# Sums of squares of the queries as one row that a transfer spreads, the last chunk's output products by heads, and the router weights' remainder ahead of GpSimd's

## The chip, the cores and the metric

The program runs on one core of a Trainium2 chip. Its time is the device time in microseconds (us) of one execution; three runs of the kernel before are shown. Less is better. The engines are TensorE (PE; PEld is its weight load), VectorE (DVE), ScalarE (ACT), GpSimd (POOL) and SyncE (SP, which here only issues transfers).

## The reference

Two layers, each cross attention and a feed-forward part, over x of 8 samples, 256 tokens, 512 features. The change lies in the second layer's attention and at the start of its feed-forward part:

```python
q = (hidden_states @ Wq + bq).reshape(b, s, NH, HD).transpose(0, 2, 1, 3)   # NH 16 heads, HD 128
k = (encoder_hidden_states @ Wk + bk) ...                                   # NKV 4 groups
q = _rmsnorm(q, qn_w)          # q * rsqrt(mean(q * q, -1) + 1e-6) * w
scores = jnp.einsum('bhsd,bhed->bhse', q, k) * scale
probs = softmax(scores)
out = jnp.einsum('bhse,bhed->bhsd', probs, v)
return out.transpose(0, 2, 1, 3).reshape(b, s, NH * HD) @ Wo
...
logits = x @ router_w.T        # the feed-forward part: 8 experts, two for each token, and a shared one
```

## The kernel before, in words

The matmuls of this attention work on float32 values that are split in two: a rounded part `hi` (float32r) and the remainder `lo`. A product is three matmuls (`matmul3`, L78 to L80: hi by lo, lo by hi, hi by hi). ScalarE makes each `hi`, VectorE or GpSimd each `lo` by a subtraction.

`ffn0_attention1` holds the first layer's feed-forward part and the second layer's attention. In the attention the 2048 tokens (16 tiles of 128) are taken in 4 chunks of 512, and the 16 heads in 4 groups of 4. The loop runs over u from 0 to 63: the groups outermost, then the chunks, then the 4 heads of the group. A head is one u; four of them make one chunk's turn in one group, after which the output is projected and added to X. There are 16 such turns, called chunks below.

Each engine's instructions stand in an order written out by hand, each behind the semaphores that it waits for. Work is staggered. At step u TensorE does: the transposes of the probabilities of head u (`transposed`, L1750), the sums of squares of head u + 2 (`square_sums`, L1718; ahead of the transposes where u is a multiple of 4), the queries of head u + 3 (`queries`, 12 matmuls of 512 columns), the scores of head u + 2 (12 of 256), the output of head u (`output`, 12 of 256), and at every fourth head the projection (`project`, 48 of 512). The projection writes to the banks that the transposes use (`ptb`), so the transposes of the next head wait until VectorE has added the last tile to X (L1560, semaphore s_added).

The path of the squares: the queries of a head lie in a PSUM bank, features on partitions, tokens in columns. ScalarE squares them (a_sq, L1360) and rounds them (a_q_hi, L1361); VectorE takes the remainder (a_q_lo, L1515). TensorE then takes each 128 columns of a_sq as weights against one column of ones, so that four matmuls (eight instructions, since they are plain float32) give the sums with tokens on partitions. VectorE copies them (a_ssq, L1520), GpSimd raises them to the power -1/2 (a_rq, L1224), and VectorE needs a_rq to scale the scores (L1528). It then takes the maxima (L1535); ScalarE the exponentials (L1367), VectorE divides (L1544), TensorE transposes, ScalarE and VectorE split the result (L1373, L1549), and TensorE multiplies by V. At every eighth head ScalarE rounds new weights (L1333 or L1341, 128x2048), and GpSimd takes their remainder (L1228 or L1234), issues the next load of weights and takes the remainder of the keys (L1241).

`feed_forward1` begins with `norm` of four tiles, then the remainder of the router's weights (L2469), both on VectorE, while GpSimd takes the remainders of the first expert's weights (L2059, L2080).

## Time and profile before

| | us |
|---|---|
| three runs: median (lowest to highest) | 1813.54 (1813.4 to 1814.91) |
| the profiled execution, its own time | 1817.25 |
| its span in the trace | 1815.5 |
| busy in the span: TensorE | 1740.2 (96%) |
| busy: VectorE | 1213.7 (67%) |
| busy: ScalarE | 851.2 (47%) |
| busy: GpSimd | 583.5 (32%) |

The profiled execution is 1.75 above its span and 3.7 above the median of the runs. The attention loop runs from 651 to 1306 in the trace. Busy time counts matmuls as the profile models them, so that matmuls that overlap are counted once; where the next one starts tells how long one holds the engine.

### The profile page before, as it was taken

The numbers are of one execution on the slowest core, as the hardware profiler recorded it, in microseconds if no ns is written. First come the engines' busy times: TensorE is split into PE (matmuls) and PEld (weight loads), VectorE is DVE, ScalarE is ACT, GpSimd is POOL, SyncE is SP. The second block draws the span as 40 slices with busy tenths as digits, with TensorE's granted clock in tenths as the row PEclk, the third lists the DMA queues.
The fourth block names the chain that finished last, engine by engine and source line by source line (L and its number), as shares of the span: only waits on it lengthen the run. The fifth ranks groups of instructions, "written<-read, shape, count | busy, mean of one in ns | idle before, by whom it ended". The sixth has DMA issues, their size and how long they took to land. (4 is left out here: it accounts for less than half of the span.)

```text
span 1815.5 us, 26738 instructions
## 1 busy us (share of the span) xinstructions
PE 1740.2 (96%) x9946; PEld 1443.8 (80%) x9966; DVE 1213.7 (67%) x2313; ACT 851.2 (47%) x1624; POOL 583.5 (32%) x441
## 2 busy tenths in 40 slices
PE   7999998996999989999999999999799999999998
PEld 6998997773444578888888888888667799999876
DVE  5444442895888777767777777777657567676555
ACT  4443432654565564445555555544341256566411
POOL 3111143224686531212132121211110245555342
PEclk9999998998999999999999999999899999999999
DMA  8323211853233761212232221110161488898573
GB/s 313 94 81 105 70 48 33 304 203 99 59 72 91 176 211 59 82 58 82 71 119 73 76 82 59 59 59 1 40 255 49 156 266 273 266 293 258 199 243 110
DMA packets 166346, 238.12 MB, mean 131 GB/s; under 512 B 42054, under 2 KB 103238, under 8 KB 164038
## 3 DMA queue, kind: packets, MB, share of 16 engines
q1 hardware_dynamic: 156620, 203.14, 34.4%
q0 software_dynamic: 9600, 33.30, 5.9%
q8 instruction: 80, 1.31, 0.3%
q14 instruction: 46, 0.38, 0.1%
HBM read 184.24 MB, written 43.78 MB: 126 GB/s over the span
## 5 line engine op out<-in xcount | busy, mean ns | idle before, releaser
L1224 POOL TENSOR_TENSOR a_rq<-a_ssq,a_qhalf 128x4 f32<-128x4 f32 x64 | 65.1, 1017 | 404.7 <-DVE a_ssq L1520 404.7
L1373 ACT ACTIVATE a_pT_hi<-bank 128x512 fp32r<-128x512 f32 x128 | 69.5, 599 | 186.1 <-PE bank L1750 185.9
L78 PE MATMUL bank<-a_xT_hi,a_wq_lo 128*128 128x512 f32 (+1 forms) x384 | 143.9, 375 | 1.4 <-DVE a_xT_lo L503 1.4
L1367 ACT ACTIVATE a_scores<-a_scores,a_nmax 128x256 f32<-128x256 f32 x256 | 127.2, 503 | 27.4 <-DVE a_nmax L1535 27.3
L80 PE MATMUL bank<-a_xT_hi,a_wq_hi 128*128 128x512 f32 (+1 forms) x384 | 138.3, 360 | 0.0
L79 PE MATMUL bank<-a_xT_lo,a_wq_hi 128*128 128x512 f32 (+1 forms) x384 | 138.1, 360 | 0.0
L78 PE MATMUL bank<-a_wo_hi,a_oT_lo 128*128 128x512 f32 x320 | 126.8, 396 | 2.9 <-DVE a_oT_lo L552 1.3
L2059 POOL TENSOR_TENSOR e_wg_lo<-raw_g,e_wg_hi 128x1408 fp32r<-128x1408 f32 x26 | 91.2, 3508 | 112.9 <-ACT e_wg_hi L2126 112.9
L1528 DVE SCALAR_TENSOR_TENSOR a_scores<-bank,a_rq,a_mask 128x256 f32<-128x256 f32 x256 | 106.1, 477 | 28.7 <-PE bank L80 20.4
L79 PE MATMUL bank<-a_wo_lo,a_oT_hi 128*128 128x512 f32 x320 | 124.9, 390 | 0.0
L80 PE MATMUL bank<-a_wo_hi,a_oT_hi 128*128 128x512 f32 x320 | 124.9, 390 | 0.0
L78 PE MATMUL bank<-a_pT_hi,a_V_lo 128*128 128x256 f32 x384 | 111.1, 289 | 8.1 <-DVE a_pT_lo L1549 6.3
L1260 POOL TENSOR_TENSOR f_h<-f_vv,f_gs 128x512 f32<-128x512 f32 x64 | 93.3, 1461 | 62.5 <-DVE f_vv L1465 61.8
L1560 DVE TENSOR_TENSOR X<-X,bank 128x512 f32<-128x512 f32 x64 | 43.8, 687 | 101.4 <-PE bank L80 101.4
L79 PE MATMUL bank<-a_pT_lo,a_V_hi 128*128 128x256 f32 x384 | 110.2, 287 | 0.0
L80 PE MATMUL bank<-a_pT_hi,a_V_hi 128*128 128x256 f32 x384 | 110.1, 287 | 0.0
L1549 DVE TENSOR_TENSOR a_pT_lo<-bank,a_pT_hi 128x512 fp32r<-128x512 f32 x128 | 82.1, 682 | 18.0 <-ACT a_pT_hi L1373 17.9
L1544 DVE TENSOR_SCALAR a_scores<-a_scores,a_rden 128x256 f32<-128x256 f32 x256 | 85.9, 399 | 2.3
L78 PEld LDWEIGHTS bank<-a_pT_hi,a_V_lo 128*128 128x128 f32 x384 | 75.1, 196 | 10.0 <-DVE a_oT_lo L1554 6.9
L80 PEld LDWEIGHTS bank<-a_xT_hi,a_wq_hi 128*128 128x128 f32 x384 | 73.7, 192 | 11.1
L78 PEld LDWEIGHTS bank<-a_xT_hi,a_wq_lo 128*128 128x128 f32 x384 | 74.1, 193 | 10.3 <-DVE a_xT_lo L503 1.8
L1535 DVE TENSOR_REDUCE a_nmax<-a_scores 128x2 f32<-128x512 f32 x128 | 81.2, 675 | 0.0
(416 smaller groups left out, 5326.2 us busy)
## 6 DMA issues: line engine op xcount, KB each, us to landing
raw_g<-in_egw SPq DMA_DIRECT2D x26, 704.0 KB, 4.7
raw_u<-in_euw SPq DMA_DIRECT2D x26, 704.0 KB, 6.2
a_xT_hi<-x1T_hi SPq DMA_DIRECT2D x16, 1024.0 KB, 6.1
a_xT_lo<-x1T_lo SPq DMA_DIRECT2D x16, 1024.0 KB, 8.5
raw_d<-in_edw SPq DMA_DIRECT2D x26, 512.0 KB, 5.9
y_routed<-m_y SPq DMA_DIRECT2D x39, 256.0 KB, 6.3
raw_d<-in_edw SPq DMA_DIRECT2D x26, 192.0 KB, 6.8
a_cTraw<-in_ctxT SPq DMA_DIRECT2D x8, 512.0 KB, 6.0
```

Source lines behind the costliest of these rows:

```text
L78: pe.matmul(out, w[1], x[0], start=first, stop=False)
L79: pe.matmul(out, w[0], x[1], start=False, stop=False)
L80: return pe.matmul(out, w[0], x[0], start=False, stop=last)
L1224: pool.tensor_tensor(rq[:, h % HG, :], ssq[:, h % HG, :], qhalf[:], ALU.pow).then_inc(s_rq, 1)
L1260: pool.tensor_tensor(h[n % 2][:, j * 512:(j + 1) * 512], vv[u % 2][:], gs[u % 2][:], ALU.mult).then_inc(s_h, 1)
L1367: act.activation(row, row, ACT.Exp, bias=nmax[:, i % 2, t:t + 1], accum_out=den[:, i % 2, t:t + 1]).then_inc(s_exp, 1)
L1373: act.activation(pT[b].hi[:], ptb[b][:].rearrange("p (k s) -> p k s", k=QT), ACT.Copy).then_inc(ft.hi, 1)
L1528: dve.scalar_tensor_tensor(sc[i % 2][:, r, :], scb[b][:, t * S:(t + 1) * S], rq[:, i % HG, r:r + 1], mask[:, t, :], ALU.mult, ALU.add).the ...
L1535: dve.tensor_reduce(nmax[:, i % 2, b * QT:(b + 1) * QT], sc[i % 2][:, b * QT:(b + 1) * QT, :], AX.X, ALU.max, negate=True).then_inc(s_nmax, 1)
L1544: dve.tensor_scalar(row, row, rden[:, i % 2, t:t + 1], None, ALU.mult).then_inc(s_p, 1)
L1549: dve.tensor_tensor(pT[b].lo[:], ptb[b][:].rearrange("p (k s) -> p k s", k=QT), f32(pT[b].hi[:]), ALU.subtract).then_inc(ft.lo, 1)
L2059: pool.tensor_tensor(pairs[w % 2].g.lo[:], raws[raw_of(w)].g[:], f32(pairs[w % 2].g.hi[:]), ALU.subtract).then_inc(s_glo, 1)
```

## The change

1. The sums of squares. The squares are themselves split: ScalarE rounds them (a_sq_hi), VectorE takes the remainder (a_sq_lo), and TensorE multiplies a single column of ones as weights by both, two matmuls of 512 columns that leave the sums as one row on one partition. ScalarE adds the epsilon and writes the row to SBUF (a_sum_row), with its columns laid so that four tokens of a partition stand together; then it issues a transfer that spreads the row over 128 partitions (a_ssq). GpSimd waits for that transfer. The sums of head u + 3 are taken at step u, between the two halves of the output of head u, and VectorE takes queries' and squares' remainders ahead of the scores.
2. The last chunk. Its projection (`project_last`) writes to banks of its own and is cut by heads: the first two heads' products ahead of the output of head 62, the third's on both sides of the output of head 63, the fourth's at the end.
3. The last layer. VectorE takes the remainder of the router's weights after one `norm` instead of four; GpSimd takes each of its first two remainders in four pieces.

```diff
         V = [first.V, over.pair("a1_V", [P, CT, HD])]
         over = Region(nc, keep.slab)
         q = [over.pair(f"a1_q{j}", [P, C]) for j in range(2)]
+        sq_lo = Region(nc, over.offset)
+        sq_lo = [sq_lo.take(f"a1_sq_lo{j}", [P, C], F32R) for j in range(2)]
         sq = [over.take(f"a1_sq{j}", [P, C]) for j in range(2)]
         K = [first.K, over.pair("a1_K", [P, C])]
...
 
         sb = lambda name, shape, dt=F32: mem.take("a1_" + name, shape, dt)
         bqg = [first.bqg, sb("bqg", [P, HG])]
-        ssq = sb("ssq", [P, HG, CT])
+        ones_r, sum_eps = sb("ones_r", [P, 1], F32R), sb("sum_eps", [P, 1])
+        ssq = [sb(f"ssq{j}", [P, CT]) for j in range(2)]
         qhalf = sb("qhalf", [P, CT])
...
 
             def rstd(u, h):
 
-                pool.wait_ge(s_ssqc, u + 1)
-                pool.tensor_tensor(rq[:, h % HG, :], ssq[:, h % HG, :], qhalf[:], ALU.pow).then_inc(s_rq, 1)
+                pool.wait_ge(s_col[u % 2], u // 2 * 16 + 16)
+                pool.tensor_tensor(rq[:, h % HG, :], ssq[u % 2][:], qhalf[:], ALU.pow).then_inc(s_rq, 1)
 
             def wq_lo(g):
...
 
             def queries(u, g, i, begin=False):
                 act.wait_ge(fq.mm, u + 1)
-                if not begin:
-                    act.wait_ge(s_ssq, u - 1)
                 if g:
                     act.wait_ge(s_bqg, g)
                 b = bqg[g % 2][:, i % HG:i % HG + 1]
+                after(act, s_ssq, u - 1)
                 act.activation(sq[i % 2][:], qb[i % 2][:], ACT.Square, bias=b).then_inc(s_sq, 1)
                 act.activation(q[i % 2].hi[:], qb[i % 2][:], ACT.Identity, bias=b).then_inc(fq.hi, 1)
+                after(act, s_ssq, u)
+                act.wait_ge(s_sq, u + 1)
+                act.activation(sq_hi[:], sq[i % 2][:], ACT.Copy).then_inc(s_sqhi, 1)
+
+            def square_sums(u):
+                act.wait_ge(s_ssq, u + 1)
+                if u:
+                    act.wait_ge(s_col[(u - 1) % 2], (u - 1) // 2 * 16 + 16)
+                act.activation(sum_row[0:1, :].rearrange("a (p t) -> a t p", t=CT),
+                               ssb[0:1, :].rearrange("a (t p) -> a t p", t=CT), ACT.Identity,
+                               bias=sum_eps[0:1, :]).then_inc(s_row, 1)
+                act.wait_ge(s_row, u + 1)
+                after(act, s_rq, u - 1)
+                act.dma_start(ssq[u % 2][:], sum_row[0:1, :].rearrange("a (p t) -> a p t", t=CT)).then_inc(s_col[u % 2], 16)
 
             def exp(u, i):
...
                         keys_hi(n + 1)
                     if i % HG == 1:
                         values_hi(n + 1)
+                if u + 3 < G * U:
+                    square_sums(u + 3)
                 output(u, n, i)
 
...
                 dve.scalar_tensor_tensor(q[i % 2].lo[:], qb[i % 2][:], bqg[u // U % 2][:, i % HG:i % HG + 1],
                                          f32(q[i % 2].hi[:]), ALU.add, ALU.subtract).then_inc(fq.lo, 1)
 
-            def square_sums(u, i):
-                dve.wait_ge(s_ssq, u + 1)
-                dve.tensor_scalar(ssq[:, i % HG, :], ssb[:, 0:CT], HD * RMS_EPS, None, ALU.add).then_inc(s_ssqc, 1)
+            def squares(u, i):
+                dve.wait_ge(s_sqhi, u + 1)
+                dve.tensor_tensor(sq_lo[i % 2][:], sq[i % 2][:], f32(sq_hi[:]), ALU.subtract).then_inc(s_sqlo, 1)
 
...
                 for t in range(CT):
                     dve.wait_ge(s_out, n * CT + t + 1)
                     row = X[:, c * CT + t, :]
-                    dve.tensor_tensor(row, row, ptb[t % 2][:], ALU.add).then_inc(s_added, 1)
+                    of = banks[t] if n == G * NC - 1 else ptb[t % 2]
+                    dve.tensor_tensor(row, row, of[:], ALU.add).then_inc(s_added, 1)
 
             def statistics(n, t):
...
             normalise(0, 0)
             for u in range(G * U):
                 i, n = u % U, u // HG
-                if u + 2 < G * U:
-                    square_sums(u + 2, i + 2)
                 transposed(u)
                 if u + 1 < G * U:
                     normalise(u + 1, i + 1)
+                if u + 3 < G * U:
+                    queries(u + 3, i + 3)
+                    squares(u + 3, i + 3)
                 if u + 2 < G * U:
                     scores(u + 2, i + 2)
-                if u + 3 < G * U:
-                    queries(u + 3, i + 3)
-                if u + 2 < G * U:
                     maxima(u + 2, i + 2)
                 if n > (G - 1) * NC:
...
                 last.then_inc(fq.mm, 1)
 
             def square_sums(u, i):
-                pe.wait_ge(s_sq, u + 1)
+                pe.wait_ge(s_sqlo, u + 1)
                 if u == 0:
                     pe.wait_ge(s_xTc, T)
-                after(pe, s_ssqc, u)
-                for t in range(CT):
-                    last = pe.matmul(ssb[:, t:t + 1], sq[i % 2][:, t * P:(t + 1) * P], ones[:, 0:1], start=True,
-                                     stop=True)
-                last.then_inc(s_ssq, 1)
+                    pe.wait_ge(s_const, 3)
+                after(pe, s_row, u)
+                pe.matmul(ssb[0:1, :], ones_r[:], sq_hi[:], start=True, stop=False)
+                pe.matmul(ssb[0:1, :], ones_r[:], sq_lo[i % 2][:], start=False, stop=True).then_inc(s_ssq, 1)
 
             def scores(u):
...
                 if u == 0:
                     pe.wait_ge(s_fadded, T)
                 after(pe, fo.lo, u)
-                for b in range(NB):
+                for b in halves:
                     pe.wait_ge(ft.lo, u * NB + b + 1)
                     for k in range(QT):
                         last = matmul3(pe, ob[:, b * S:(b + 1) * S], part(v, slice(None), b * QT + k),
                                        part(pT[b], slice(None), k), k == 0, k == QT - 1)
-                last.then_inc(fo.mm, 1)
+                if NB - 1 in halves:
+                    last.then_inc(fo.mm, 1)
 
             def project(u, n):
...
                                 last.then_inc(s_out, 1)
+
+            def project_last(heads, tiles):
+
+                pe.wait_ge(fo.lo, G * U - HG + heads[-1] + 1)
+                for t in tiles:
+                    for k in heads:
+                        last = matmul3(pe, banks[t][:], part(oT, slice(None), k, slice(t * P, (t + 1) * P)),
+                                       part(wo, slice(None), k), k == 0, k == HG - 1)
+                    if HG - 1 in heads:
+                        last.then_inc(s_out, 1)
 
             x_transposed(0)
...
             next_xT(T - 1)
             for u in range(G * U):
                 g, i, n = u // U, u % U, u // HG
-                if i % HG == 0 and u + 2 < G * U:
-                    square_sums(u + 2, i + 2)
                 transposed(u, n, i)
-                if i % HG and u + 2 < G * U:
-                    square_sums(u + 2, i + 2)
                 if u + 3 < G * U:
                     queries(u + 3)
                 if u + 2 < G * U:
                     scores(u + 2)
-                output(u)
-                if i % HG == HG - 1:
+                if u == G * U - 2:
+                    pe.wait_ge(s_masked, G * U * CT)
+                    project_last(range(HG - 2), range(CT))
+                if u == G * U - 1:
+                    project_last(range(HG - 2, HG - 1), range(CT // 2))
+                output(u, range(1))
+                if u + 3 < G * U:
+                    square_sums(u + 3, i + 3)
+                output(u, range(1, NB))
+                if u == G * U - 1:
+                    project_last(range(HG - 2, HG - 1), range(CT // 2, CT))
+                    project_last(range(HG - 1, HG), range(CT))
+                elif i % HG == HG - 1:
                     if i == HG - 1:
                         pe.wait_ge(s_wolo, g + 1)
...
             pool.affine_select(out=before[:], in_=ones[:], compare_op=ALU.is_gt, fill=0.0, base=0,
                                pattern=[[1, P]], channel_multiplier=-1).then_inc(s_const, 1)
             pool.tensor_tensor(fold[:], ident[0:2 * E, 0:E], ident[0:2 * E, E:2 * E], ALU.add).then_inc(s_fold, 1)
-            gate_lo(0)
+            pool.wait_ge(s_ghi, 1)
+            for k in range(KD):
+                ins = pool.tensor_tensor(pair0.g.lo[:, k, :], raw0.g[:, k, :], f32(pair0.g.hi[:, k, :]), ALU.subtract)
+            ins.then_inc(s_glo, 1)
             pool.wait_ge(s_uhi, 1)
-            pool.tensor_tensor(pair0.u.lo[:], raw0.u[:], f32(pair0.u.hi[:]), ALU.subtract).then_inc(s_ulo, 1)
+            for k in range(KD):
+                ins = pool.tensor_tensor(pair0.u.lo[:, k, :], raw0.u[:, k, :], f32(pair0.u.hi[:, k, :]), ALU.subtract)
+            ins.then_inc(s_ulo, 1)
             pool.wait_ge(s_ve, 1)
             pool.tensor_tensor(rstd[:, T - CT:T], last.ve[:, T - CT:T], last.mhalf[:, T - CT:T], ALU.pow).then_inc(s_rstd, 1)
...
                 step(dve.tensor_tensor(tokf[:], tokf[:], tb[0][:, NT:2 * NT], ALU.add))
                 dve.tensor_copy(token[:], tokf[:]).then_inc(s_tok, 1)
 
-            for t in chunk(0):
-                norm(t)
+            norm(0)
             dve.wait_ge(s_rw, 1)
             dve.tensor_tensor(rw2[:, :, E:2 * E], rw[:], f32(rw2[:, :, 0:E]), ALU.subtract).then_inc(s_rw, 1)
+            for t in range(1, CT):
+                norm(t)
             transposed(0)
             transposed(1)
```

The order of the instructions on three engines, read from the two programs; L numbers of the changed kernel are its own.

VectorE, inside the attention loop (`ffn0_attention1`), the steps of one head of the kernel before, from the scores of one head to the output of the previous:

```order
L1528 SCALAR_TENSOR_TENSOR a_scores_4403<-bank,a_rq,a_mask 128x256 x4
L1515 SCALAR_TENSOR_TENSOR a_q_lo<-bank,a_bqg,a_q_hi 128x512
L1535 TENSOR_REDUCE a_nmax<-a_scores_4403 128x2 x2
L1554 TENSOR_TENSOR a_oT_lo<-bank,a_oT_hi 128x512
L1520 TENSOR_SCALAR a_ssq<-bank 128x4
L1549 TENSOR_TENSOR a_pT_lo<-bank,a_pT_hi 128x512 x2
L1540 RECIPROCAL a_rden<-a_den 128x4
L1544 TENSOR_SCALAR a_scores_4403<-a_scores_4403,a_rden 128x256 x4
```

And in the changed kernel, the same stretch of VectorE:

```order
L1544 SCALAR_TENSOR_TENSOR a_q_lo<-bank,a_bqg,a_q_hi 128x512
L1549 TENSOR_TENSOR a_sq_lo_4410<-a_sq_4412,a_sq_hi 128x512
L1557 SCALAR_TENSOR_TENSOR a_scores_4403<-bank,a_rq,a_mask 128x256 x4
L1564 TENSOR_REDUCE a_nmax<-a_scores_4403 128x2 x2
L1583 TENSOR_TENSOR a_oT_lo<-bank,a_oT_hi 128x512
L1578 TENSOR_TENSOR a_pT_lo<-bank,a_pT_hi 128x512 x2
L1569 RECIPROCAL a_rden<-a_den 128x4
L1573 TENSOR_SCALAR a_scores_4403<-a_scores_4403,a_rden 128x256 x4
```

The copy of the sums (a_ssq) is gone, the remainder of the next queries (a_q_lo) has moved ahead of the scores, and the remainder of their squares (a_sq_lo) stands behind it.

TensorE, the steps of one head in the kernel before (rows of the middle of each run of products left out; a_scores are transposed first, then come the sums, the queries, the scores, the output):

```order
L1750 MATMUL bank<-ident,a_scores_4403 128x128 x8
L1718 MATMUL bank<-ones,a_sq_4411 128x1 x4
L78 MATMUL bank<-a_xT_hi,a_wq_lo 128x512
...
L78 MATMUL bank<-a_K_hi,a_q_lo 128x256
...
L78 MATMUL bank<-a_pT_hi,a_V_lo 128x256
```

And in the changed kernel, from the scores to the next head's transposes:

```order
L78 MATMUL bank<-a_K_hi,a_q_lo 128x256
...
L78 MATMUL bank<-a_pT_hi,a_V_lo 128x256
...
L1747 MATMUL bank<-a_sq_hi,a_ones_r 1x512
L1748 MATMUL bank<-a_sq_lo_4410,a_ones_r 1x512
L78 MATMUL bank<-a_pT_hi,a_V_lo 128x256
...
L1778 MATMUL bank<-ident,a_scores_4402 128x128 x8
```

The sums of squares of head u + 3 now stand between the two halves of the output of head u, eighteen matmuls behind the queries that they are summed from; before, those of head u + 2 stood right behind the transposes, a whole head after their queries.

ScalarE, the steps of one head in the kernel before:

```order
L1379 ACTIVATE a_oT_hi<-bank 128x512
L1373 ACTIVATE a_pT_hi<-bank 128x512 x2
L1367 ACTIVATE a_scores_4402,a_den<-a_scores_4402,a_nmax 128x256 x4
L1360 ACTIVATE a_sq_4410<-bank,a_bqg 128x512
L1361 ACTIVATE a_q_hi<-bank,a_bqg 128x512
```

And in the changed kernel:

```order
L1401 ACTIVATE a_oT_hi<-bank 128x512
L1395 ACTIVATE a_pT_hi<-bank 128x512 x2
L1389 ACTIVATE a_scores_4403,a_den<-a_scores_4403,a_nmax 128x256 x4
L1368 ACTIVATE a_sq_4413<-bank,a_bqg 128x512
L1369 ACTIVATE a_q_hi<-bank,a_bqg 128x512
L1372 ACTIVATE a_sq_hi<-a_sq_4413 128x512
L1378 ACTIVATE a_sum_row<-bank,a_sum_eps 1x4x128
L1383 DMA a_ssq_4428<-a_sum_row 128x1x4
```

Three steps are new: the rounded squares (a_sq_hi), the row of sums out of its bank (a_sum_row), and the issue of the transfer that spreads the row over the partitions.

## Rows read from the trace of the kernel before

**Rows 1.** Windows: stretch and length, busy time of each engine, TensorE clock, DMA.
```profile
655.00:1272.00 617.00, 615.10 (x3842) 548.27 (x3841) 458.62 (x1036) 319.37 (x818) 136.37 (x103) 1.00 0.22 74
```

**Rows 2.** Timeline of TensorE (start, us, engine, line): one head, projection, next head.
```profile
1003.97 1.04 PE L1750 MATMUL bank<-ident,a_scores 128*128 128x128 f32 x8
1004.84 0.95 PE L1718 MATMUL bank<-ones,a_sq 128*128 128x1 f32 x8
1005.65 0.48 PE L78 MATMUL bank<-a_xT_hi,a_wq_lo 128*128 128x512 f32 x1
...
1008.24 0.39 PE L80 MATMUL bank<-a_xT_hi,a_wq_hi 128*128 128x512 f32 x1
1008.47 0.28 PE L78 MATMUL bank<-a_K_hi,a_q_lo 128*128 128x256 f32 x1
...
1011.32 0.40 PE L78 MATMUL bank<-a_wo_hi,a_oT_lo 128*128 128x512 f32 x1
...
1022.63 0.95 PE L1718 MATMUL bank<-ones,a_sq 128*128 128x1 f32 x8
1023.58 1.09 PE L1750 MATMUL bank<-ident,a_scores 128*128 128x128 f32 x8
```

**Rows 3.** Timeline of ScalarE in the head that starts at 1023.58.
```profile
1024.27 1.09 ACT L1373 ACTIVATE a_pT_hi<-bank 128x512 fp32r<-128x512 f32 x2 [12.15 <-PE bank L1750]
...
1027.47 0.69 ACT L1360 ACTIVATE a_sq<-bank,a_bqg 128x512 f32<-128x512 f32 x1 [0.15 <-PE bank L80]
1028.05 0.68 ACT L1361 ACTIVATE a_q_hi<-bank,a_bqg 128x512 fp32r<-128x512 f32 x1
1028.62 0.63 ACT L1346 ACTIVATE a_K_hi<-ahead_ctx 128x512 fp32r<-128x512 f32 x1
```

**Rows 4.** Timeline of VectorE around the same head.
```profile
1022.15 1.38 DVE L1560 TENSOR_TENSOR X<-X,bank 128x512 f32<-128x512 f32 x2 [4.48 <-PE bank L80]
...
1027.56 1.14 DVE L1544 TENSOR_SCALAR a_scores<-a_scores,a_rden 128x256 f32<-128x256 f32 x4
...
1030.54 0.74 DVE L1515 SCALAR_TENSOR_TENSOR a_q_lo<-bank,a_bqg,a_q_hi 128x512 fp32r<-128x512 f32 x1
1031.20 1.27 DVE L1535 TENSOR_REDUCE a_nmax<-a_scores 128x2 f32<-128x512 f32 x2
```

**Rows 5.** Groups of instructions: count, then busy time and mean ns of one.
```profile
L2285 DVE TENSOR_TENSOR e_wd_lo<-raw_d,e_wd_hi 96x512 fp32r<-96x512 f32 x25 | 16.9, 678 | 0.0
```

**Rows 6.** Timeline of SyncE: start and length of one DMA issue.
```profile
1030.65 0.34 SPq L1144 DMA_DIRECT2D ahead_ctx<-K  x1
```

**Rows 7.** DMA issues: count, KB each, median us to landing.
```profile
r_rw<-in_rwT SPq DMA_DIRECT2D x1, 16.0 KB, 1.8
ahead_ctx<-K SPq DMA_DIRECT2D x16, 256.0 KB, 5.6
```

**Rows 8.** Timeline of GpSimd at two starts of eight heads.
```profile
660.37 4.61 POOL L1234 TENSOR_TENSOR a_wo_lo<-ahead_raw,a_wo_hi 128x2048 fp32r<-128x2048 f32 x1 [7.52 <-ACT a_wo_hi L1341]
...
666.12 1.30 POOL L1241 TENSOR_TENSOR a_K_lo<-ahead_ctx,a_K_hi 128x512 fp32r<-128x512 f32 x1
...
1159.88 1.05 POOL L1224 TENSOR_TENSOR a_rq<-a_ssq,a_qhalf 128x4 f32<-128x4 f32 x1
```

**Rows 9.** Timeline of VectorE at the same two places.
```profile
664.46 3.11 DVE L1544 TENSOR_SCALAR a_scores<-a_scores,a_rden 128x256 f32<-128x256 f32 x4
...
1158.10 2.49 DVE L1544 TENSOR_SCALAR a_scores<-a_scores,a_rden 128x256 f32<-128x256 f32 x4
```

**Rows 10.** One line of ScalarE: duration ns min/median/max, first and last start.
```profile
L1333 ACT ACTIVATE a_wq_hi<-ahead_raw x3: 1917/1917/1920, 740.6 to 1069.7; 128x2048 fp32r<-128x2048 f32 x3
```

**Rows 11.** Timeline of TensorE in the last three heads: its waits.
```profile
1287.48 0.55 PE L78 MATMUL bank<-a_pT_hi,a_V_lo 128*128 128x256 f32 x1 [4.06 <-DVE a_pT_lo L1549]
```

**Rows 12.** Timelines of VectorE and GpSimd at the start of the last layer.
```profile
1309.63 3.17 DVE L2469 TENSOR_TENSOR r_rw<-r_rw,r_rw 128x32 fp32r<-128x32 f32 x1
...
1309.36 3.40 POOL L2059 TENSOR_TENSOR e_wg_lo<-raw_g,e_wg_hi 128x1408 fp32r<-128x1408 f32 x1 [0.50 <-ACT e_wg_hi L2126]
```

34 lines of the change are left out of this document (24 added, 10 removed).

## The prediction

> **What bounds the kernel now.** I read the page first, then the stretch of the attention loop, then one head on each engine. TensorE is busy in 615.1 of the 617 us of the loop and its clock stands at 1.00, that is 2.4 GHz [rows 1], so there the time is what TensorE issues, and any wait that it gets is added in full. The timeline shows one head: transposes at 1003.97, sums of squares at 1004.84, queries at 1005.65, scores at 1008.47, output behind them, projection at 1011.32 [rows 2]. A head is 1011.32 - 1003.97 = 7.35, of it the sums 0.81, the twelve matmuls of the queries 2.82 (0.235 each), scores and output 2.85 together; both are twelve matmuls of 256 columns, so 1.43 each. The projection is 1022.63 - 1011.32 = 11.31. A chunk is 4 x 7.35 + 11.31 + 0.14 (the sums take 0.95 where they come first) = 40.85. In the last three heads there are true waits, 4.06 the longest [rows 11].
>
> **The sums themselves.** Removed: 0.81 a head (0.95 in a chunk's first). Added: two matmuls of 512 columns. With one column as weights they are not in the trace; I take the 0.235 of a 512-column matmul with 128, so 0.47. Bounds: 0.2 if half went by, 0.81 if plain float32 were the nearer row. TensorE's own work falls by 0.34 a head, 22 over 64 heads.
>
> **The wait that comes with them.** Now the sums of head u + 3 stand eighteen matmuls behind its queries, and they need the remainder of the squares. I count from E, the end of the last matmul of the queries, 1008.24 + 0.39 = 1008.63 [rows 2]. The scores start at 1008.47 and take 1.43, half an output 0.71: TensorE reaches the sums at 1010.61, E + 1.98. The chain beside it: ScalarE starts the squares about 0.05 after a matmul ends (the hand-over in the other direction is as short: the last addition ends at 1022.15 + 1.38 = 1023.53, the transposes start at 1023.58 [rows 2, 4]); a_q_hi starts 0.58 behind the squares and takes 0.68 [rows 3], so it ends at E + 1.31. VectorE's a_q_lo starts at E + 1.36, the next instruction follows 0.66 later [rows 4], and a_sq_lo, a subtraction in SBUF, takes 0.68 [rows 5]: E + 2.70. With 0.1 for the weight load ahead of the matmul, E + 2.80. The rounding of the squares on ScalarE (0.63, as a_K_hi from SBUF, behind 0.57 of a_q_hi [rows 3]) ends at E + 1.8 and decides nothing. So TensorE waits 2.80 - 1.98 = 0.82 in each head, with every engine free in time. Behind it on TensorE stand the second half of the output and the next transposes, and ScalarE and VectorE wait for those, so nothing catches it up. Bounds 0.6 to 1.0, from hand-overs of 0 to 0.1. A head becomes 7.35 - 0.81 + 0.47 + 0.82 = 7.83.
>
> **The chunk's first head.** Its transposes wait for the last addition, which ends at 1023.53 [rows 4]; today the sums (1022.63 to 1023.58 [rows 2]) fill just that time. With the sums gone from there the wait is bare: 0.95, no gain. A chunk is 0.95 + 4 x 7.83 + 11.31 = 43.58, that is 2.73 more.
>
> **The issue on ScalarE.** ScalarE must wait for its own row (0.68, as the other steps with a bias [rows 3]), then issue the transfer. No row has an issue on ScalarE; SyncE's shortest near here is 0.34 [rows 6], GpSimd's issues cost more, and the lower bound is nothing. I take 0.34. From the start S of the sums: they end at S + 0.63, the row ends at S + 1.36, the issue at S + 1.75, a_oT_hi holds ScalarE 0.5 more, so a_pT_hi starts at S + 2.25. It could have started 0.69 (1024.27 - 1023.58) behind the transposes [rows 2, 3], which start at S + 0.47 + 0.71, so at S + 1.87: 0.38 late. From a_pT_hi to the end of the division takes 1027.56 + 1.14 - 1024.27 = 4.43 [rows 3, 4], and a_q_lo stands behind it; this way it starts about 0.25 later than by the queries. That adds 0.25 to three heads of a chunk, 0.75. A chunk is then 44.3, 3.5 more; over fifteen chunks +52. Nothing for the issue gives +41; an issue of 0.8 gives +21 more.
>
> **Every eighth head.** GpSimd's subtraction of new weights, the load and the keys hold it from 660.37 to 667.42, 7.05 in all [rows 8], and VectorE's division there takes 3.11 instead of 1.14, ending 0.15 behind GpSimd [rows 9]. Today this costs TensorE some tenths, since the probabilities are needed a head later. Afterwards the squares stand behind that division. Counted from the transposes: the rounding of the weights (1.92 [rows 10]) starts at 5.7, GpSimd goes from 7.6 to 14.7, the next head's division is due at 7.83 + 3.98 = 11.8 [rows 2, 4] and is held to 14.7; 0.8 for its rest, 0.66, 0.68 and 0.1 bring the squares to 16.9, where TensorE wants them at 7.83 + 6.65 = 14.5. That is 2.4; less about 0.3 that I grant for today's cost it is 2.1, seven times: +15. Bounds 0 to 4 each.
>
> The Trainium skill, SBUF - State Buffer, "Who interferes with whom", says that a VectorE instruction with two SBUF inputs contends with a GpSimd instruction that reads SBUF, and that the later one is blocked until the other ends. The trace agrees: 3.17 us for 32 columns beside GpSimd's 3.40 [rows 12]. By that rule a_sq_lo could also be held by a_rq, once a head.
>
> **The transfer.** Its 2 KB have no like here. The column's transfer starts at S + 1.75; VectorE wants a_rq behind a_sq_lo, about 6.7 behind the next transposes, S + 7.9. Less 1.05 of a_rq [rows 8], 5.1 is left for landing. Rows bound it by 1.8 (16 KB) and 5.6 (256 KB) [rows 7]; it is nearer in size to the first. Cost nothing; past 5.1 it is charged.
>
> **The ends.** In the last chunk 24 matmuls (5.6) of the projection go where the 4.06 wait is, less 1.6 that they overshoot and 1.4 (a_oT_hi and its remainder ahead of the last head's products), with a lesser wait filled: about -2 (0 to -5). The router's remainder leaves the shadow of GpSimd's 3.40 and drops from 3.17 to 0.2, part of it on the path: -2.5 (0 to -4). The loop's start I leave at 0, between -3 and +3.
>
> **Sum.** 52 + 15 - 2 - 2.5 = +62.5. The profiled execution took 1817.25, which gives 1879.8; it stands 3.7 above the median, so 1876.
>
> **Rivals.**
> *Cheap edges*: the issue costs ScalarE nothing and the eighth heads half: +62.5 - 11 - 7.5, about 1857. For it: most issues have no engine waiting; against it: ScalarE here has a wait on itself ahead. It shares the forecast's mechanism.
> *A late column or a blocked remainder*: a landing of 8 us in the one head of a chunk beside the 2 MB loads puts VectorE 2.9 late, of which some 0.9 is slack: 2 x 15 = +30, 1906. If a_rq held a_sq_lo or the division for its full 1.0 in each head, 61 more, 1937. Against the last: at a later start the divisions ended at 1160.59 while a_rq ran from 1159.88 to 1160.93 [rows 8, 9], so it did not hold them.
> *Faster, the remainder is hidden*: if a_sq_lo were ready by E + 1.98, the chain being 0.82 shorter than its rows, a head is 7.01 and a chunk 0.95 + 28.0 + 11.31 = 40.3, 0.55 less than now: -8, and -4.5 at the ends, 1801. It needs hand-overs and durations below every row; the sign turns where the wait is under about 0.2 and issue and eighth heads cost nothing.
> *The change does nothing measurable*: 1813, only by chance between these.
>
> **How the numbers follow.** Forecast 0.68, cheap edges 0.15, late or blocked 0.12, faster 0.03, no change 0.02. The time is the forecast's, 1876. The range: below, cheap edges with waits of 0.66 instead of 0.82 (-10), 1847; above, an issue of 0.8, 1897, widened to 1900. So slower 0.95, within 0.2% 0.02, faster 0.03; 0.2% (3.6 us) is about what a measurement can tell here.
>
> **What would show it.** TensorE's wait ahead of the first sums matmul, put down to a_sq_lo, near 0.8 in chunk-first heads and near 1.1 in the others, 50 to 70 us in all; the sums 0.23 apart; a chunk of about 44.3, every second 2.5 longer; transposes of each chunk's first head waiting 1.0 for X. Wrong, if those waits are missing, if a_ssq lands past 5 us, or if TensorE's clock falls from 1.00 at waits this short.

## The result, and the profile after

| | runs | median, us (lowest to highest) |
|---|---|---|
| before | 4 | 1814.22 (1813.4 to 1815.51) |
| after | 4 | 1913.1 (1911.03 to 1917.66) |

The ratio is 1.0547, with a 95% interval of 1.0533 to 1.0561: 99 us more, where the prediction had 62.5 more and a range that ended at 1900. The span of the profiled execution is 1912.6.

The stretch of the attention loop, in the view that [rows 1] show for before (length, then busy time of PE, PEld, DVE, ACT and POOL, the clock, DMA), from the changed kernel:

```profile
660.00:1365.00 705.00, 607.05 (x3437) 512.25 (x3437) 488.04 (x1027) 410.86 (x927) 139.72 (x103) 0.97 0.20 63
```

TensorE now has 98 us without work in this stretch, and its clock is no longer at 1.00 throughout. The chain of waits in the loop says for what (engine and line that waited, releaser, us in total, times, longest):

```profile
POOL a_rq L1232 <- DMA a_ssq<-a_sum_row: 365.0, 56, 19.8
...
ACT a_sum_row L1378 <- PE bank L1748: 89.7, 54, 3.5
PE bank L1747 <- DVE a_sq_lo L1549: 89.6, 62, 4.0
DVE a_rden L1569 <- ACT a_scores L1389: 64.7, 62, 1.3
...
ACT a_oT_hi L1401 <- ACT a_sum_row L1378: 30.8, 54, 0.6
...
PE bank L1778 <- DVE X L1590: 11.7, 15, 0.8
...
DVE a_scores L1557 <- POOL a_rq L1232: 3.0, 3, 1.9
```

The second to fourth lines are three engines waiting for one another in turn: TensorE for the remainder of the squares, ScalarE for TensorE's sums, VectorE for ScalarE's exponentials. GpSimd's 365 us for the column are idle time of an engine that nobody waits for: VectorE waited for a_rq only 3.0 us in all. TensorE's timeline, the sums in a chunk's first and second head and in its fourth (start, us, engine, line; the wait is in brackets):

```profile
1043.94 0.39 PE L1747 MATMUL bank<-a_sq_hi,a_ones_r 128*1 128x512 f32 x1 [0.61 <-DVE a_sq_lo L1549]
...
1054.81 0.59 PE L1747 MATMUL bank<-a_sq_hi,a_ones_r 128*1 128x512 f32 x1 [3.74 <-DVE a_sq_lo L1549]
...
1073.45 0.39 PE L1747 MATMUL bank<-a_sq_hi,a_ones_r 128*1 128x512 f32 x1 [1.52 <-DVE a_sq_lo L1549]
1073.68 0.40 PE L1748 MATMUL bank<-a_sq_lo,a_ones_r 128*1 128x512 f32 x1
```

The last pair, 1.52, is what the second to fourth heads of an ordinary chunk show. The line ahead of it, 3.74, stands in the second head of a chunk in which GpSimd takes the remainder of new weights; the matmul behind it takes 0.59 instead of 0.39. ScalarE in the same fourth head:

```profile
1070.65 0.68 ACT L1368 ACTIVATE a_sq<-bank,a_bqg 128x512 f32<-128x512 f32 x1
1071.22 0.69 ACT L1369 ACTIVATE a_q_hi<-bank,a_bqg 128x512 fp32r<-128x512 f32 x1
1071.79 0.64 ACT L1372 ACTIVATE a_sq_hi<-a_sq 128x512 fp32r<-128x512 f32 x1
1074.12 1.18 ACT L1378 ACTIVATE a_sum_row<-bank,a_sum_eps 1x512 f32<-1x512 f32 x1 [1.69 <-PE bank L1748]
1075.32 0.48 ACTq L1383 DMA_DIRECT2D a_ssq<-a_sum_row  x1
1075.84 0.60 ACT L1401 ACTIVATE a_oT_hi<-bank 128x512 fp32r<-128x512 f32 x1 [0.55 <-ACT a_sum_row L1378]
```

The row, 512 numbers on one partition, takes 1.18, not the 0.68 of the other steps with a bias [rows 3], and its issue 0.48. From the starts of TensorE's transposes (L1778; before L1750) come the lengths of heads and chunks, worked out by subtraction for this kernel and for those of the experiments. The prediction's "every eighth head" is the third column: every second chunk, in whose first head ScalarE rounds 128x2048 new weights and GpSimd takes their remainder. Its range covers five such chunks; the first and the thirteenth (47.2 in the changed kernel, 40.9 before) are apart:

```
                     heads of an ordinary chunk   chunk   a chunk with GpSimd's   first
                     (fourth: with projection)            large remainders        chunk
before               6.57  7.41  7.41  19.67      41.07   41.2                    43.5
after                7.76  8.70  8.65  20.90      46.0    49.6                    52.5
row written plainly  7.76  8.17  8.12  20.37      44.4    48.8 to 50.0            47.8
issue by SyncE       7.76  7.93  7.92  20.15      43.75   49.0 to 50.5            52.8
sums later           7.06  8.68  8.63  20.86      45.2    47.5 to 48.3            51.2
no remainder         6.78  6.74  6.75  18.99      39.3 *  42.0                    42.2
pieces               7.78  8.71  8.64  20.88      46.0    49.9 to 51.3            51.4
four moves           7.06  7.10  7.07  19.32      40.5    45.9 to 47.9            49.6
  and spread         7.07  7.08  7.07  19.30      40.5    41.6 to 42.6            44.0
  no rem. and spread 6.79  6.78  6.75  19.03      39.35   39.3 to 40.2            42.0
  the same, earlier  6.79  6.78  6.75  19.03      39.35   39.3                    41.4
* 39.3 to 40.2
```

The fifteen chunks up to head 60 are together 97.1 longer than before, and so are the spans (1912.6 - 1815.5): the loss lies in the loop. Eight ordinary chunks are 4.9 to 5.1 longer, five with large remainders 8.4 to 8.5, the first 9.1, the thirteenth 6.3.

### The profile page after: what moved, and what is told of

Read it like the earlier page. It is cut to its first block and busy times, and to the rows that moved or that the text cites. A ratio compares the mean times of both kernels' runs of the same rounds, so it can differ in the third digit from the quotient of the medians.

```text
span 1912.6 us, 26422 instructions
## 1 busy us (share of the span) xinstructions
PE 1739.3 (91%) x9562; PEld 1410.8 (74%) x9582; DVE 1245.4 (65%) x2313; ACT 953.2 (50%) x1753; POOL 588.3 (31%) x448
## 3 DMA queue, kind: packets, MB, share of 16 engines
q8 instruction: 78, 1.28, 0.3%
## 5 line engine op out<-in xcount | busy, mean ns | idle before, releaser
L1378 ACT ACTIVATE a_sum_row<-bank,a_sum_eps 1x512 f32<-1x512 f32 x64 | 76.2, 1190 | 89.7 <-PE bank L1748 89.7
L1747 PE MATMUL bank<-a_sq_hi,a_ones_r 128*1 128x512 f32 x64 | 26.6, 415 | 90.7 <-DVE a_sq_lo L1549 90.7
L1778 PE MATMUL bank<-ident,a_scores 128*128 128x128 f32 x512 | 74.1, 292 | 14.3 <-DVE X L1590 11.7
```

What stands on the lines that cost most here:

```text
L1378: act.activation(sum_row[0:1, :].rearrange("a (p t) -> a t p", t=CT), ssb[0:1, :].rearrange("a (t p) -> a t p", t=CT), ACT.Identity, bias= ...
L1778: last = pe.transpose(ptb[b][:, k * S + t * P:k * S + (t + 1) * P], sc[i % 2][:, r, k * P:(k + 1) * P], ident[:])
```

## The experiments

Theory A is the prediction's: TensorE waits for a_sq_lo, and what ScalarE does for the row stands ahead of a_oT_hi and a_pT_hi, so that an edge there comes round to the next head's squares. Theory B is that the transfer of the column, or GpSimd's power of -1/2 behind it (a_rq), is late. Theory C is that GpSimd's hold on VectorE and the slower clock make most of the loss. All runs are given beside runs of the kernel before on the same chip (1814.5, 1817.5, 1815.2 and 1815.4 us in the four groups).

**The other two parts alone** (the kernel before with `project_last`, the router's order and GpSimd's pieces).

> The kernel before with the change's other two parts alone: the last chunk's output products split by heads, and the router's remainder ahead of GpSimd's pieces; the sums of squares stay as they were. Both theories on the loss lay it on the sums, so both expect this kernel slightly under the kernel before: the forecast's terms were -2 (0 to -5) for the tail and -2.5 (0 to -4) for the router, so 1810 us against 1814, ratio 0.9975. If the two parts cost something that the loop hid, it would be at or over 1814.

Measured: 1810.71 us, ratio 0.9986 (0.9975 to 0.9996), so these parts gain 0.7 to 4.5 us (0.0004 to 0.0025 of 1814). The loss is the sums' alone. The router's remainder, which took 3.17 beside GpSimd [rows 12], takes 0.28 now; the line is the changed kernel's:

```profile
L2520 DVE TENSOR_TENSOR r_rw<-r_rw,r_rw 128x32 fp32r<-128x32 f32 x1 | 0.3, 278 | 0.0
```

**The row written plainly.**

```diff
-act.activation(sum_row[0:1, :].rearrange("a (p t) -> a t p", t=CT),
-               ssb[0:1, :].rearrange("a (t p) -> a t p", t=CT), ACT.Identity,
+act.activation(sum_row[0:1, :].rearrange("a (p t) -> a p t", t=CT),
+               ssb[0:1, :].rearrange("a (t p) -> a p t", t=CT), ACT.Identity,
```

> The changed kernel with the row written as it comes and the bank read in steps of four elements' order instead (the same row lands in the same place in the buffer; only which side of ScalarE's instruction has the stride is changed). Theory A (what ScalarE does for the row stands ahead of a_oT_hi, and each part of it is paid in three heads of four): if the strided write made the row 1.19 us instead of 0.68, the row falls by 0.51 and 47 heads by as much: 1913 - 24 = 1889 us. If the row stays at 1.19, the stride of the write is not the cause, and the time stays at 1913. Theory B (the column's landing or the power behind it is late): the row ends 0.5 us earlier and nothing else changes, so the time stays at 1913 whatever the row takes. Theory C (GpSimd's hold and the clock): 1913 too.

Measured: 1898.88 us, ratio 1.0468 (1.0451 to 1.0486). The group of the row, of this kernel and then of the changed one (count, busy time, mean ns of one, idle time ahead):

```profile
L1378 ACT ACTIVATE a_sum_row<-bank,a_sum_eps 1x512 f32<-1x512 f32 x62 | 42.0, 678 | 96.0 <-PE bank L1748 96.0
```

```profile
L1378 ACT ACTIVATE a_sum_row<-bank,a_sum_eps 1x512 f32<-1x512 f32 x62 | 73.9, 1191 | 89.7 <-PE bank L1748 89.7
```

678 ns against 1191: the write in steps of 16 bytes costs 0.51 us; a read of PSUM in steps of 512 bytes costs nothing. Second, third and fourth heads are 0.53 shorter each, first heads not at all, as theory A says; for theory B nothing should have moved. A chunk is 44.4, and the forecast with 0.68 for the row was 44.3. Of the 24 us expected 14 came (22 in the profiled execution, the shortest of the four): in the chunks with large remainders the gain was lost again, since the first of VectorE's four division steps was held until GpSimd's a_K_lo ended and the fourth until its a_V_lo ended:

```profile
1035.88 4.07 DVE L1573 TENSOR_SCALAR a_scores<-a_scores,a_rden 128x256 f32<-128x256 f32 x4
```

The Trainium skill, SBUF — State Buffer, "Door 1: The DMA port swizzle", states that SBUF has lines of 16 bytes and that each access that crosses to a new line pays a penalty. The trace agrees: the strided write, four float32 apart, takes 1.76 times the plain one (1191 / 678).

**The transfer issued by SyncE.**

```diff
 # ScalarE, square_sums(u): heads 0 to 2 keep their issue there
-act.wait_ge(s_row, u + 1)
-after(act, s_rq, u - 1)
-act.dma_start(ssq[u % 2][:], ...)
 # SyncE
+for u in range(G * U - 3):
+    sp.wait_ge(s_row, u + 4)
+    sp.wait_ge(s_rq, u + 2)
+    sp.dma_start(ssq[(u + 3) % 2][:], ...)
+    ...   # x behind the first head's, K behind the second's, V behind the third's
```

> The changed kernel with the transfers of heads 3 and on issued from SyncE's queue; the loads of keys, values and x that SyncE issues are put between them. Theory A: ScalarE goes from the row straight to a_oT_hi, which stands 0.55 to 0.6 us behind it now; 47 heads are shorter by 0.55 to 0.6: 1913 - 27 = 1886 us. The row itself stays at 1.19. Theory B (the landing is what is late): the column lands at best at the same time, more likely 0.1 to 0.3 us later for the step to another engine, so 1913 to 1925. Theory C: 1913.

Measured: 1891.95 us, ratio 1.0426 (1.0408 to 1.0445). ScalarE now goes on at once:

```profile
1054.44 1.20 ACT L1391 ACTIVATE a_sum_row<-bank,a_sum_eps 1x512 f32<-1x512 f32 x1 [1.58 <-PE bank L1761]
1055.43 0.63 ACT L1414 ACTIVATE a_oT_hi<-bank 128x512 fp32r<-128x512 f32 x1
```

a_oT_hi starts 0.99 behind the row's start, where it stood 1.72 behind it (1075.84 - 1074.12). So waiting for its own row and issuing cost ScalarE 0.73, and the second to fourth heads are shorter by 0.72 to 0.77, the first heads by nothing. That is more than the 0.55 to 0.6 expected: a_oT_hi, which waits for nothing here, starts 0.21 before the row ends (1055.43 against 1055.64). The chunks with large remainders gave some of it back, so that 21 us came instead of 27.

**The sums later on TensorE.**

```diff
-output(u, range(1))
+output(u, range(NB))
 if u + 3 < G * U:
     square_sums(u + 3, i + 3)
-output(u, range(1, NB))
```

> The changed kernel with TensorE's sums behind all six of a head's remaining output products (0.72 us later in its order) instead of ahead of them; ScalarE's order is as it was. If TensorE's wait for a_sq_lo is itself the cost, the products cover it: 0.6 of 15 first heads and 0.72 of 47 others are gained, 1913 - 9 - 34 = 1870 us. Theory A in its full form says that the other heads run in a loop through ScalarE (a_sq_lo, sums, row, issue, a_oT_hi, a_pT_hi, exponentials, squares, a_sq_lo) in which the products have no part: only the first heads of chunks gain 0.6, 1913 - 9 = 1904 us, and TensorE's wait for a_sq_lo shrinks while one of the same size shows elsewhere. Theory B: 1913 or more.

Measured: 1895.46 us, ratio 1.0445 (1.0427 to 1.0463). This run tells the two forms of theory A apart. First heads gain 0.70; the three others gain nothing (8.68, 8.63, 20.86), although six more products now stand ahead of the sums. TensorE's timeline in a fourth head:

```profile
1061.77 0.40 PE L1747 MATMUL bank<-a_sq_hi,a_ones_r 128*1 128x512 f32 x1 [1.50 <-DVE a_sq_lo L1549]
```

The wait is 1.50 as before, just one place later. In these heads the products are not what sets the time. The loop is: a_sq_lo, the sums, the row and its issue, a_oT_hi, a_pT_hi, the exponentials, and from there VectorE's division and a_q_lo to the next a_sq_lo. It closes through VectorE: in the changed kernel's fourth head above, a_sq_hi ends at 1072.43, and a_sq_lo starts behind a_q_lo at 1072.72. The 9 us beyond the 1904 expected lie in the chunks with large remainders, 47.5 to 48.3 instead of 49.6.

**Without the squares' remainder.**

```diff
-act.activation(sq_hi[:], sq[i % 2][:], ACT.Copy)       # ScalarE; a_sq is written rounded now
-dve.tensor_tensor(sq_lo[i % 2][:], sq[i % 2][:], f32(sq_hi[:]), ALU.subtract)
-pe.matmul(ssb[0:1, :], ones_r[:], sq_hi[:], start=True, stop=False)
-pe.matmul(ssb[0:1, :], ones_r[:], sq_lo[i % 2][:], start=False, stop=True)
+pe.matmul(ssb[0:1, :], ones_r[:], sq[i % 2][:], start=True, stop=True)
```

> The changed kernel without the squares' remainder: ScalarE writes the square rounded at once, a_sq_hi and a_sq_lo are gone, and one matmul sums. What it leaves out: the part of each square below TensorE's rounding. The row, its strided write (1.19 us) and its issue stay on ScalarE. Theory A: the sums no longer wait (the square ends before the fourth product), so 1.52 us goes in each of 47 heads, 0.6 in 15 first heads and about 3 in 7 eighth heads: 1913 - 70 - 9 - 20 = 1814 us, about the kernel before, though row and issue still cost what they cost. Theory B (landing and power late): the row is only earlier, and VectorE's scores are not waiting for it now, so 1913. Theory C (GpSimd's hold and the clock): a_sq_lo is one of the instructions that are held, so the eighth heads alone gain: 1913 - 10 to 20.

Measured: 1810.4 us, ratio 0.997 (0.9951 to 0.9988). The row still takes 1186 ns and is still issued by ScalarE, and neither costs anything in ordinary heads now: once a_sq_lo is gone the loop no longer closes and TensorE is the bound. The run takes out more than the loop's edge: one matmul a head (0.23, some 15 us in all), and a step each of ScalarE and VectorE. TensorE's timeline has the sums without a wait and heads of 6.74:

```profile
1031.90 1.04 PE L1773 MATMUL bank<-ident,a_scores 128*128 128x128 f32 x8
1037.69 0.39 PE L1743 MATMUL bank<-a_sq,a_ones_r 128*1 128x512 f32 x1
1038.64 1.04 PE L1773 MATMUL bank<-ident,a_scores 128*128 128x128 f32 x8
```

Theory B is refuted here and theory C as the main cause: this kernel sends the same transfers and has GpSimd's same work.

**GpSimd's large remainders in pieces** (each 128x2048 subtraction of `wq_lo` and `wo_lo` as four of 128x512 behind one another).

> The changed kernel with GpSimd's remainders of 128x2048 (4.6 us each) in four pieces of 128x512 behind one another. The term under test is that of the eighth heads (chunks of 49.6 us beside 46.0, seven of them: 25 us, and the first chunk of 52.5). If VectorE gets in between two pieces, its division and a_sq_lo lose about 1.2 us at most instead of up to 4, the 3.7 us waits fall to 2 and the clock stays up: chunks of 46.5 to 47.5, 1913 - 18 = 1895 us. If pieces behind one another hold VectorE as one instruction does: 1913, and chunks stay at 49.6.

Measured: 1916.81 us, ratio 1.055 (1.0532 to 1.0568). Nothing is gained. VectorE beside the four pieces, then GpSimd:

```profile
1047.46 1.27 DVE L1568 TENSOR_REDUCE a_nmax<-a_scores 128x2 f32<-128x512 f32 x2
1050.35 1.28 DVE L1582 TENSOR_TENSOR a_pT_lo<-bank,a_pT_hi 128x512 fp32r<-128x512 f32 x2
```

```profile
1046.99 5.04 POOL L1245 TENSOR_TENSOR a_wo_lo<-ahead_raw,a_wo_hi 128x512 fp32r<-128x512 f32 x4 [16.10 <-ACT a_wo_hi L1354]
1052.33 0.80 POOL L1249 DMA_DIRECT2D ahead_raw<-in_Wq  x1 [0.30 <-POOL a_wo_lo L1245]
1053.15 1.28 POOL L1253 TENSOR_TENSOR a_K_lo<-ahead_ctx,a_K_hi 128x512 fp32r<-128x512 f32 x1
1054.38 1.10 POOL L1232 TENSOR_TENSOR a_rq<-a_ssq,a_qhalf 128x4 f32<-128x4 f32 x1
1055.46 1.25 POOL L1257 TENSOR_TENSOR a_V_lo<-ahead_ctx,a_V_hi 128x512 fp32r<-128x512 f32 x1
```

The pieces hold nothing: the maxima and a_pT_lo take beside them what they take elsewhere, and the changed kernel's one subtraction of 4.62 us stood beside the same steps. The division comes behind it, and meets the remainders of K and V. Its first step, its first three and all four, from the same timeline with narrower windows:

```profile
1052.89 1.71 DVE L1577 TENSOR_SCALAR a_scores<-a_scores,a_rden 128x256 f32<-128x256 f32 x1
1052.89 2.23 DVE L1577 TENSOR_SCALAR a_scores<-a_scores,a_rden 128x256 f32<-128x256 f32 x3
1052.89 3.98 DVE L1577 TENSOR_SCALAR a_scores<-a_scores,a_rden 128x256 f32<-128x256 f32 x4
```

The first step ends at 1054.60, 0.17 behind a_K_lo; the second and third pass beside a_rq in 0.34 each; the fourth ends at 1056.87, 0.16 behind a_V_lo. By the Trainium skill, SBUF — State Buffer, "Who interferes with whom", the one that is issued second is blocked for the other's whole instruction. The trace agrees: each hold ends with the one instruction of GpSimd that it met, and a_rq holds nothing. So cutting the large subtraction could not help here. What it does is push a_K_lo and a_V_lo back to where VectorE divides and takes a_sq_lo, and four pieces behind one another push them as far (5.04 us against 4.62). Whether pieces hold VectorE less where they do meet it, this run does not show.

**Four moves together**: the three above and the row behind a_oT_hi on ScalarE.

```diff
+output(u, n, i)
 if u + 3 < G * U:
     square_sums(u + 3)
-output(u, n, i)
```

> The changed kernel with the three edits tried singly (the row written plainly, the transfer issued by SyncE, the sums behind the head's last product) and a fourth: the row stands behind a_oT_hi on ScalarE instead of ahead of it. Theory A: with the row out of the loop, TensorE waits only for a_sq_lo, 0.1 us; VectorE's own work of some 7.2 us a head is then the longest; heads of 7.1, 7.3, 7.3 and about 19.6, chunks of 41.3, the eighth ones 3 more: 1814 + 15 x 0.2 + 7 x 3 + 5 = 1843 us. If each saving went with its own singly measured share (-19, -22 and -18), it would be 1913 - 59 = 1854. Theory B: the column lands some 1.2 us later in the head than before this edit, so scores wait for a_rq and the time is over 1880.

Measured: 1853.15 us, ratio 1.0197 (1.018 to 1.0214). Ordinary chunks are 40.5, less than the 41.07 of before: the row is out of the loop, and the heads of 7.1 are now about as long as VectorE's own work, which runs through the second and third without a gap. What is left lies in the chunks with large remainders, 46 to 48, more than expected (1843 us was), and in the fourteenth and fifteenth, 43.6 each, where VectorE also takes the last layer's statistics.

**The four moves without the remainder.**

> The kernel with all four moves, without the squares' remainder as well (left out: the part of each square below TensorE's rounding). Theory A: nothing of the sums stands in TensorE's way; a head has 0.57 us less of products and ScalarE and VectorE have 0.5 and 0.6 less each; TensorE is the bound again, only the wait for X's addition (0.8 to 0.95 in a chunk's first head) is no longer filled by 0.81 us of sums: chunks of 39.4 to 39.9 beside 41.07, some 20 us under the kernel before, about 1790. Theory B: over 1814, since the landing would be late here at the latest.

Measured: 1804.12 us, ratio 0.9925 (0.9905 to 0.9944). Ordinary chunks are 39.35, just under the 39.4 to 39.9 expected; those with large remainders are 40.2 to 42.0, which the expectation of 1790 had left out. Beside the run without the remainder alone, the four moves gain 6 us more.

**GpSimd's remainders spread**: pieces over three heads, each behind that head's a_sq_lo (or a_q_lo).

```diff
+if u + 3 < G * U:
+    pool.wait_ge(s_sqlo, u + 4)
 ...                                   # K's and V's remainders stay here
+pieces = (range(0), range(1), range(1, 3), range(3, 4))[i % HG]
+if i < HG and len(pieces):
+    wo_lo(g, pieces)
+if U // 2 <= i < U // 2 + HG and g + 1 < G and len(pieces):
+    wq_lo(g + 1, pieces)
```

> The kernel with all four moves, and GpSimd's remainders spread: each 128x2048 one in pieces of 128x512 over three heads (one, two, one), and every piece, K's and V's too, behind that head's a_sq_lo, so that it runs beside VectorE's scores and maxima, which read PSUM or were not held in the traces so far. Its chunks without GpSimd's large work are 40.5 us (before: 41.06), the seven with it 46 to 48, the first 49.6. Theory A with GpSimd's hold as the cause of the eighth heads' term: those fall to 40.5 to 42: 1853 - 7 x 5.5 - 5 = 1810 us, under the kernel before by 4. If the term is another one (ScalarE's a_wo_hi of 1.9 us ahead of a_oT_hi, or the slow clock by itself), chunks stay at 44 or over and the time at 1840 or more. Theory B (the landing): 1853, nothing changes for it.

Measured: 1820.49 us, ratio 1.003 (1.002 to 1.0041). The chunks with large remainders fall from 46 to 48 to 41.6 to 42.6: the spread takes away most of their excess over 40.5. Two things went together in it. In the kernel with the four moves VectorE's division and a_sq_lo are held for 22 us in all beside a_K_lo and a_V_lo, here for nothing; and the clock no longer falls. The run does not tell them apart. Two pieces beside VectorE's scores and maxima, of GpSimd and then of VectorE:

```profile
1002.74 2.54 POOL L1260 TENSOR_TENSOR a_wo_lo<-ahead_raw,a_wo_hi 128x512 fp32r<-128x512 f32 x2 [1.56 <-DVE a_sq_lo L1573]
```

```profile
1001.98 0.68 DVE L1573 TENSOR_TENSOR a_sq_lo<-a_sq,a_sq_hi 128x512 fp32r<-128x512 f32 x1
1002.57 1.66 DVE L1581 SCALAR_TENSOR_TENSOR a_scores<-bank,a_rq,a_mask 128x256 f32<-128x256 f32 x4
1004.14 1.27 DVE L1588 TENSOR_REDUCE a_nmax<-a_scores 128x2 f32<-128x512 f32 x2
```

VectorE's durations are those of a head without GpSimd. A stretch of 600 us of this kernel's loop has the clock at 1.00:

```profile
660.00:1260.00 600.00, 574.12 (x3364) 484.45 (x3363) 458.48 (x1005) 374.38 (x921) 137.85 (x123) 1.00 0.23 74
```

It misses the 1810 expected. What it loses against before lies in its fourteenth and fifteenth chunks of 42.9, where VectorE also has the last layer's statistics, and in those with pieces, 0.4 to 1.7 longer than before's; in four of these TensorE waits for the last piece of a_wo_lo (2.9 us in all) and the fourth head takes 20.3 instead of 19.3. That the statistics are the cause was not tried.

**The same spread without the remainder of the squares.**

> The same spread in the kernel with all four moves and without the squares' remainder (left out: the part of each square below TensorE's rounding); the pieces stand behind a_q_lo, there being no a_sq_lo. Its seven chunks of 40.2 to 42.0 should fall to 39.4 to 39.8 as their neighbours: 1804 - 7 x 2.2 - 3 = 1786 us. If GpSimd's hold is not what makes them long: 1804.

Measured: 1794.29 us, ratio 0.9887 (0.9871 to 0.9903), 10 us gained by the spread where 18 were expected. Three of the chunks with pieces are 39.3, three 40.2 to 40.3; in these and in the first the projection waits for the last piece of a_wo_lo (a fourth head of 19.9 to 20.0 instead of 19.0).

**The spread in the kernel as changed, and nothing else.**

> The changed kernel with nothing but that spread of GpSimd's remainders. If GpSimd's hold on VectorE is the term of the eighth heads, their chunks fall from 49.6 to 46.0 to 46.8 and the first from 52.5 to 49: 1913 - 7 x 3.2 - 3 = 1888 us; what is left to 1814 is then theory A's alone, some 4.9 us in each chunk. Theory C (GpSimd's hold and the clock make most of the loss): the time falls by over 50, to 1860 or less.

Measured: 1899.48 us, ratio 1.0457 (1.044 to 1.0474). It gains 14, not 25 and not over 50: theory C is worth this much of the 99. Chunks with large remainders are 46.7 to 47.6, not 49.6.

What made them 49.6 can be read from the changed kernel's trace, here in the second head of one. The rounding of the weights and a_oT_hi on ScalarE, with a_oT_hi of an ordinary chunk's second head:

```profile
1042.91 1.91 ACT L1350 ACTIVATE a_wo_hi<-ahead_raw 128x2048 fp32r<-128x2048 f32 x1
1047.03 0.60 ACT L1401 ACTIVATE a_oT_hi<-bank 128x512 fp32r<-128x512 f32 x1 [0.61 <-ACT a_sum_row L1378]
1095.94 0.60 ACT L1401 ACTIVATE a_oT_hi<-bank 128x512 fp32r<-128x512 f32 x1 [0.61 <-ACT a_sum_row L1378]
```

GpSimd, and VectorE beside it:

```profile
1044.90 4.62 POOL L1242 TENSOR_TENSOR a_wo_lo<-ahead_raw,a_wo_hi 128x2048 fp32r<-128x2048 f32 x1 [16.08 <-ACT a_wo_hi L1350]
1050.64 1.28 POOL L1249 TENSOR_TENSOR a_K_lo<-ahead_ctx,a_K_hi 128x512 fp32r<-128x512 f32 x1
1052.95 1.25 POOL L1253 TENSOR_TENSOR a_V_lo<-ahead_ctx,a_V_hi 128x512 fp32r<-128x512 f32 x1
1050.80 2.07 DVE L1573 TENSOR_SCALAR a_scores<-a_scores,a_rden 128x256 f32<-128x256 f32 x4
1053.45 1.30 DVE L1549 TENSOR_TENSOR a_sq_lo<-a_sq,a_sq_hi 128x512 fp32r<-128x512 f32 x1
```

The window behind the wait of 3.74, in which TensorE's clock is 0.50, that is 1.2 GHz:

```profile
1054.80:1059.80 5.00, 4.99 (x19) 4.39 (x20) 4.27 (x9) 3.23 (x6) 0.72 (x1) 0.50 0.31 96
```

Counted from the head's transposes (1045.12; 1094.65 in the ordinary chunk), a_oT_hi starts at 1.91 instead of 1.29: 0.62 late. The division takes 0.93 longer, held by a_K_lo; a_sq_lo takes 0.62 longer, held by a_V_lo; and at the lower clock TensorE needs 2.09 instead of 1.18 from the sums to the next transposes (1056.90 - 1054.81). Together 3.1, the head's 11.8 against 8.7. The third head is 0.5 longer, its first products still at the lower clock.

**Pieces a head earlier.** `(range(1), range(1, 2), range(2, 4), range(0))`.

> The kernel with all four moves, the spread and no remainder of the squares (left out as before: the part of each square below TensorE's rounding), with one change more: GpSimd's pieces of the large remainders stand in the chunk's first three heads (one, one, two) instead of the second to fourth, so that the products of the output weights no longer wait for the last piece. In the trace of the kernel with pieces in the second to fourth heads that wait is 4.6 us in four places, and four of its fourth heads take 20.0 instead of 19.0. Expected: those four fall by 0.9 to 1.0, 1794 - 4 = 1790 us; if the earlier pieces hold VectorE in a first head instead, where ScalarE already rounds weights for 1.9 us, it stays at 1794.

Measured: 1789.2 us, ratio 0.9853 (0.9837 to 0.987), as expected and the fastest here. The second to thirteenth chunks are 39.3, the fourteenth and fifteenth 40.2. It leaves out the squares' remainder; of the kernels that keep it, only the one with the two other parts alone is under the kernel before.

## Why the prediction was right in kind and short in size

- **The sums themselves**: right. L1747 and L1748 start 0.23 apart, 0.46 a head for the two.
- **The wait for a_sq_lo**: 0.82 forecast for every head with the engines free in time; 0.61 where that holds, in first heads (a head of 7.76 to 7.82 against the forecast's 7.83).
- **The chunk's first head**: its transposes wait for X bare, as forecast (0.78 on TensorE in 15 chunks, with the weight load ahead of it).
- **The issue on ScalarE: this is the step that failed, in its size.** It took "0.68, as the other steps with a bias" for the row and 0.34 for the issue, and made 0.25 in three heads of it. The row took 1.19 and the issue 0.48 on ScalarE; the second and third heads are 0.85 to 0.94 longer than the first, where 0.25 + 0.51 + 0.14 makes 0.90. The wait for a_sq_lo in these heads was 1.5, not the 1.1 that the prediction named. The mechanism stood: with the row at 0.68 a chunk was 44.4 (forecast 44.3), with it at 1.19 it is 46.0. Over fifteen chunks an ordinary chunk's excess is 15 x 4.93 = 74 where 52 was forecast: 22 of the 34.6 us missed. The bound of an issue of 0.8 guarded the wrong side of the step: the row had been given no range.
- **Every eighth head**: +15 forecast with bounds of 0 to 4 each; measured 3.5 in each of five chunks, 4.1 in the first and 1.3 in the thirteenth, 23 in all: 8 more. The place was right, the working was not. The forecast had the division due 11.8 behind the first head's transposes and held to 14.7, through all that GpSimd does in a row. It started at 13.5 and lost 0.93 to a_K_lo alone: a hold lasted as long as the one instruction that it met. What it left out makes up for that and more: the row late by 0.62 behind ScalarE's rounding of the weights, a_sq_lo held by V's remainder (1.30 instead of 0.68), and some 1.4 at the lower clock behind the 3.74 wait. The clock is 0.97 over the stretch, where the forecast had 1.00: it fell in seven such chunks, at waits of 2.2 to 4.1, and at none of 1.5. That the term came out within its bounds of 0 to 4 is in part luck.
- **The transfer**: right. It landed 2.0 us behind its issue, and 5.1 was free.
- **The ends**: -4.5 forecast, and -0.7 to -4.5 measured alone. In the changed kernel they come to nothing: the loop starts 0.7 later, its end from head 60 on takes 0.9 more, and from the last addition to the end of the span it is 507.6 instead of 509.2, 1.6 less.
- **The sum**: 74 + 23 + 0 = 97, the difference of the two spans; 22 + 8 + 4.5 = 34.5 is what the forecast of 62.5 lacked. Of the rivals, the late column did not happen; nor did a_rq hold anything: three a_sq_lo that started while it ran took 0.68, and 28 division steps 0.34 to 0.35. The cheap edges were the reverse of the truth. The chance of 0.95 for slower was sound; the range was too narrow, since the row had no bound and the upper bound of the eighth heads (13 more) was not put into it.

## What to carry to other kernels

A step that is put on an engine ahead of work that others wait for is paid in full, and again in each round, if it closes a loop between engines. So look for the loop (engines that wait for one another in turn, by like amounts), and break it at one place: here dropping the remainder was worth 103 us (some 15 of them for the matmul that went too), three moves of its other parts, made singly, 14 to 21 each, and all four moves together, the row out of the loop, 60. When moving an instruction off a loop, write it plainly first: look at the steps of its write, not only at its number of elements. Work of GpSimd that reads SBUF belongs beside VectorE instructions that read PSUM or reduce, with a wait that puts it there. Before cutting a long GpSimd instruction, look at which one VectorE really meets, step by step: here it was the short ones behind it.
